# Sorting 65,536 edges by source on packed words: 15 of 16 merges of a bitonic sort carry one word per edge instead of two

## The chip, the cores and the metric

The kernel runs on one core of one Trainium2 chip. The metric is the device time of one execution in microseconds (us), the median of several executions. Engines are named as in the profile: PE (TensorE), DVE (VectorE), ACT (ScalarE), POOL (GpSimd), SP (SyncE, which here only issues DMAs).

## The reference

Four graph layers are applied one after another to node features `x` (100,000 nodes, 64 features) over 50,000 edges (`src`, `dst`, with `dst` sorted), each as `x = x + layer(relu(layernorm(x)))`. The second of them needs a softmax over the edges that share a *source*:

```python
src, dst = (edge_index[0], edge_index[1])
e = jax.nn.leaky_relu(h[src] @ a_src + h[dst] @ a_dst, ALPHA)
seg_max = jax.ops.segment_max(e, src, num_segments=num_nodes)
exp_e = jnp.exp(e - seg_max[src])
denom = jax.ops.segment_sum(exp_e, src, num_segments=num_nodes)
attention = exp_e / denom[src]
h_prime = jax.ops.segment_sum(attention[:, None] * h[src], dst, num_segments=num_nodes)
```

The edges arrive sorted by `dst`, so the kernel sorts them by `src` itself.

## The kernel before, in words

The program is a chain of blocks. A block opens a set of tiles and semaphores, gives each engine its own list of instructions, and ends with a barrier of all engines; nothing of the next block starts before it. The first block, `prologue_block` (tiles named `su_...`), prepares indices and weights. The second is `gat_block` "a" (tiles `a_...`), which gathers node rows by edge; its first instructions are the DMAs of SP at L712 and L717 and POOL's gathers at L755.

Inside the prologue, four strands run side by side:

- **DVE** first prepares masks (L268 to L306, L564 to L568) and then sorts. The sort is a bitonic network over `SORTED` = 65,536 slots, in tiles of 128 partitions by `SF` = 512 columns. `key` holds the source, `pay` the number of the edge, both as fp32, each in two copies used in turn. Merge k (k = 1 to 16) has k exchanges, 136 in all. Ahead of each merge a header of four instructions over 128x512 (L342 to L345) flips the keys' signs where the merge runs downwards, so that every exchange is the same: smaller value to the front. Each exchange is seven instructions over 128x256 (L325 to L331): a comparison and a difference of payloads, a minimum and a maximum of the keys, the product of comparison and difference, and two that move the payloads by it.
- **PE and ACT** serve the merges above 9 (`inner`), whose wide exchanges cross partitions. `turn_tiles` (L336) signals PE, which transposes `key` into the bank `bk` and `pay` into `bp` (L539), ACT copies both back (L526, L527), and DVE goes on. Each of the merges 10 to 16 has two such turns, 14 in all.
- **POOL** issues 392 indirect DMAs (L403), each of which scatters 128 single words into the table `XL`. They wait for masks of DVE (`dv`), and for the copy of the node table into `XL` (`xlc`). There are no data between them and the sort.
- **SP and ACT** issue loads and stores. SP stores the sorted keys and edge numbers (L464, L465) when DVE has signalled `sorted_` (L356), and then 18 small DMAs of weight parts (L471).

The block ends when all strands have ended: for DVE that is L383, behind the sort; for POOL the landing of its last scatter.

`ch(...)` is a helper: the instruction increments a semaphore, and DVE waits for that value before it goes on. In an exchange there are three such waits (behind L326, L329 and L331), in a header four.

Of the kernel before, what the change touches and what calls it, by code (L numbers as in the profile page):

```python
# [5 lines left out]
ALU = mybir.AluOpType  # L6
ACT = mybir.ActivationFunctionType
F32 = mybir.dt.float32
I32 = mybir.dt.int32
# [3 lines left out]
P = 128  # L13
N, D = 100000, 64
# [14 lines left out]
SORTED = 1 << (E - 1).bit_length()  # L29
SF = SORTED // P  # L30
SLAST = E - (P - 1) * EF
XW = D + 2
FAR = 1 << 23

# [158 lines left out]
def prologue_block(nc, a, T, C):  # L193

    with ExitStack() as ctx:
# [43 lines left out]
        tmp = [m.sb(f"tmp{i}", [P, SF // 2]) for i in range(3)]  # L239
        sign = m.sb("sign", [P, SF])  # L240
        bits = m.sb("bits", [P, SF], I32)
        place = m.sb("place", [P, SF], I32)
        srcs = m.sb("srcs", [P, SF], I32)
        eid = m.sb("eid", [P, SF], I32)
# [22 lines left out]
        def _(dve):  # L267
# [2 lines left out]
            nc.vector.memset(dstn[:, :], N)  # L270
            nc.vector.memset(C["at"][:, 0, EF - J:EF], 0)
            nc.vector.memset(C["at"][:, 1, EF - J:EF], N - 1)
            nc.vector.memset(sign[:, :], 1.0)
            nc.vector.memset(srcs[:, :], SKIP)
            nc.vector.memset(beyond[:, :], SKIP)
            nc.vector.memset(ewp[:, :], 0.0)
            nc.vector.memset(etp[:, :], 0)
# [32 lines left out]
            ch = Chain(dve, s_sort, 0)  # L310
            ch.at(0)
            dve.wait_ge(s_seed, 1)
            ch(v.tensor_copy(pay[0][:, :], place[:, :]))
            dve.wait_ge(s_ld, 16 * 2)
            dve.wait_ge(pads, 1)
            ch(v.tensor_copy(key[0][:, :], srcs[:, :]))
            cur, nt_, half = 0, 0, SORTED // P // 2

            def exchange(cur, d):
                a_ = lambda t: t[:, :].rearrange("p (g two d) -> p g two d", two=2, d=d)  # L320
                h_ = lambda t: t[:, :].rearrange("p (g d) -> p g d", d=d)
                ka, kb = a_(key[cur])[:, :, 0, :], a_(key[cur])[:, :, 1, :]
                pa, pb = a_(pay[cur])[:, :, 0, :], a_(pay[cur])[:, :, 1, :]
                nk, np_ = a_(key[1 - cur]), a_(pay[1 - cur])
                v.tensor_tensor(h_(tmp[0]), ka, kb, ALU.is_gt)  # L325
                ch(v.tensor_tensor(h_(tmp[1]), pb, pa, ALU.subtract))  # L326
                v.tensor_tensor(nk[:, :, 0, :], ka, kb, ALU.min)
                v.tensor_tensor(nk[:, :, 1, :], ka, kb, ALU.max)
                ch(v.tensor_tensor(tmp[2][:, :], tmp[0][:, :], tmp[1][:, :], ALU.mult))  # L329
                v.tensor_tensor(np_[:, :, 0, :], pa, h_(tmp[2]), ALU.add)  # L330
                ch(v.tensor_tensor(np_[:, :, 1, :], pb, h_(tmp[2]), ALU.subtract))  # L331
                return 1 - cur

            def turn_tiles(cur, n):

# [3 lines left out]

            for k in merges:  # L340

                ch(v.tensor_scalar(bits[:, :], place[:, :], k, 1, ALU.logical_shift_right, ALU.bitwise_and))  # L342
                ch(v.tensor_tensor(key[cur][:, :], key[cur][:, :], sign[:, :], ALU.mult))
                ch(v.tensor_scalar(sign[:, :], bits[:, :], -2.0, 1.0, ALU.mult, ALU.add))
                ch(v.tensor_tensor(key[cur][:, :], key[cur][:, :], sign[:, :], ALU.mult))  # L345
                if k > inner:
                    nt_ = turn_tiles(cur, nt_)
                    for j in range(k - 1, inner - 1, -1):
                        cur = exchange(cur, 1 << (j - inner))
                    nt_ = turn_tiles(cur, nt_)  # L350
                for j in range(min(k, inner) - 1, -1, -1):
                    cur = exchange(cur, 1 << j)

            if cur:
                ch(v.tensor_copy(key[0][:, :], key[1][:, :]))
# [120 lines left out]
        @block.scalar  # L476
        def _(act):
            act.wait_ge(pads, 1)
            act.dma_start(srcs[0:full, :], a["src"][0:full * SF].rearrange("(p f) -> p f", f=SF)).then_inc(s_ld, 16)
            act.dma_start(srcs[full:full + 1, 0:E - full * SF], a["src"][full * SF:E].unsqueeze(0)).then_inc(s_ld, 16)  # L480
            for c in range(1, 10, 2):
                act.dma_start(wide_rows(T["XL"], c), wide_rows(a["nodes"], c)).then_inc(xlc, 16)
            loads_ = 0

            def load(dst, src):
                act.dma_start(dst, src).then_inc(wl, 16)
                return 1
# [24 lines left out]
            for q in range(2):  # L512
                loads_ += load(C["a1"][:, q:q + 1], a["L1_gnn_a"][0, q * D:(q + 1) * D].unsqueeze(1))
            for q in range(4):
                loads_ += load(C["wflat"][:, q % 2, q // 2, :],
                          a["L2_gnn_weight"].rearrange("b i o -> (b i o)").rearrange("(q p i) -> q p i", p=P, i=D)[q])
            comp = a["w_comp_t"]
            for r in range(4):
                for q in range(4):
                    loads_ += load(C["cstk"][32 * r + 8 * q:32 * r + 8 * q + 8, 16 * q:16 * q + 16], comp)  # L520
            for name, of, H, W in (("att1b", "L0_gnn_att1", 8, 16), ("att2b", "L0_gnn_att2", 2, 64), ("att3b", "L3_gnn_att", 4, 16)):
                for h in range(H):
                    loads_ += load(C[name][h * W:(h + 1) * W, h:h + 1], a[of][h].unsqueeze(1))
            for n, cur in enumerate(current_at_turns()):
                act.wait_ge(s_tp, n + 1)
                nc.scalar.activation(key[cur][:, :], bk[:, :], ACT.Copy)  # L526
                nc.scalar.activation(pay[cur][:, :], bp[:, :], ACT.Copy).then_inc(s_tr, 1)  # L527
            act.wait_ge(wl, 16 * loads_)
            act.sem_inc(s_wr, 1)

        @block.tensor
        def _(pe):
            pe.wait_ge(s_id, 1)
            for n, cur in enumerate(current_at_turns()):
                pe.wait_ge(s_tq, n + 1)
                for tile_, bank in ((key[cur], bk), (pay[cur], bp)):
                    for b in range(SF // P):

                        last = nc.tensor.transpose(bank[:, b * P:(b + 1) * P], tile_[:, b * P:(b + 1) * P], C["ident"][:, :])  # L539
                last.then_inc(s_tp, 1)  # L540

            pe.wait_ge(s_ab, 1)
            for q in range(2):
                nc.tensor.matmul(pw[:, q * D:(q + 1) * D], ab[:, q, :], C["w1"][:, :], start=True, stop=True)
            nc.tensor.transpose(pt[:, :], C["w1"][:, :], C["ident"][0:D, 0:D])
            for q in range(2):
                last = nc.tensor.transpose(pf[:, q, :], C["wflat"][:, q, :, :].rearrange("p c i -> p (c i)"), C["ident"][:, :])
            last.then_inc(s_pe, 1)
# [1654 lines left out]
```

## Time and profile before

| | |
|---|---|
| median of 3 executions | 9188.93 us (9160.83 to 9189.82) |
| the profiled execution | 9215.03 us, of which the span is 9213.2 us |
| busy share of the span | DVE 70%, POOL 49%, PE 48%, ACT 31% |
| prologue block | 0 to 918.7 us of the span |
| DVE at 104.7 us | first instruction of the sort (L313) |
| DVE at 901.1 us | last instruction of the sort (L356) |

How to read it: the shares are means over 13 blocks with a barrier between each two. The change touches the first block alone, so what counts is which strand of that block ends last.

### The profile page before, as it was taken

The numbers are of one execution on the slowest core, as the hardware profiler recorded it, in microseconds if no ns is written. First come the engines' busy times: TensorE is split into PE (matmuls) and PEld (weight loads), VectorE is DVE, ScalarE is ACT, GpSimd is POOL, SyncE is SP. The second block draws the span as 40 slices with busy tenths as digits, with TensorE's granted clock in tenths as the row PEclk, the third lists the DMA queues.
The fourth block names the chain that finished last, engine by engine and source line by source line (L and its number), as shares of the span: only waits on it lengthen the run. The fifth ranks groups of instructions, "written<-read, shape, count | busy, mean of one in ns | idle before, by whom it ended". The sixth has DMA issues, their size and how long they took to land. (4 is left out here: it accounts for less than half of the span.)

```text
span 9213.2 us, 91644 instructions
## 1 busy us (share of the span) xinstructions
PE 4455.8 (48%) x13072; PEld 2477.6 (27%) x13072; DVE 6495.0 (70%) x20579; ACT 2837.8 (31%) x6952; POOL 4503.7 (49%) x4361
## 2 busy tenths in 40 slices
PE   0000556565566565776000988867756676720000
PEld 0000222222233333665000546623323333310000
DVE  4227789888576776877566998767868787878422
ACT  0000344443122222555343000134434444457200
POOL 3760666664666664554554000055445565623566
PEclk9999766666677766555555997578865555555555
DMA  5000333334333331111453002566634444433222
GB/s 150 1 1 4 73 78 84 79 79 69 74 73 73 72 74 41 36 36 46 88 100 81 1 4 83 146 109 128 127 79 88 88 92 84 94 99 123 74 79 74
DMA packets 910191, 686.98 MB, mean 75 GB/s; under 512 B 599695, under 2 KB 748972, under 8 KB 909450
## 3 DMA queue, kind: packets, MB, share of 16 engines
q1 hardware_dynamic: 515806, 377.81, 15.5%
q0 software_dynamic: 137984, 138.92, 12.0%
q10 hardware_dynamic: 256232, 168.62, 5.9%
q14 instruction: 138, 1.13, 0.0%
q8 instruction: 31, 0.51, 0.0%
HBM read 491.06 MB, written 227.24 MB: 78 GB/s over the span
## 5 line engine op out<-in xcount | busy, mean ns | idle before, releaser
L755 POOL DMA_INDIRECT a_xg<-t_XL,c_at x784 | 808.5, 1031 | 741.9 <-issue 292.6
L755 POOL DMA_INDIRECT g_xg<-t_D,c_at x784 | 784.2, 1000 | 630.8 <-DMA t_HN<-g_hn 305.9
L755 POOL DMA_INDIRECT b_xg<-t_H,c_at x784 | 815.5, 1040 | 494.1 <-issue 242.8
L1740 POOL DMA_INDIRECT f_dg<-t_D,c_at x392 | 371.3, 947 | 1286.7 <-POOLq L175 974.3
L1088 POOL DMA_INDIRECT t_RANK<-m_place,m_at x392 | 386.2, 985 | 393.9 <-DMA m_place<-t_POS 285.8
L1273 POOL DMA_INDIRECT l_d<-t_D,l_ix x392 | 387.8, 989 | 318.4 <-DVE l_xs L1289 136.8
L403 POOL DMA_INDIRECT t_XL<-su_pos,su_scatx x392 | 405.1, 1033 | 245.2 <-DMA t_XL<-in_nodes 126.1
L2108 POOL DMA_INDIRECT out<-o_y,o_ix x392 | 385.9, 984 | 260.7 <-issue 209.5
L539 PE MATMUL su_bk<-c_ident,su_key 128*128 128x128 f32 x56 | 15.6, 434 | 847.9 <-DVE su_tmp L336 847.9
L1010 PE MATMUL g_bank<-g_zt,c_att3r 64*128 64x512 f32 x196 | 200.1, 1123 | 414.1 <-DVE g_zt L800 238.1
L1322 ACT ACTIVATE l_hn<-l_xs,l_sm 128x64 f32<-128x64 f32 x784 | 265.0, 426 | 429.1 <-DVE l_sm L631 348.0
L1010 PE MATMUL a_bank<-a_zt,c_att1r 128*128 128x512 f32 x196 | 200.3, 1126 | 405.7 <-issue 217.0
L1010 PE MATMUL b_bank<-b_zt,c_att2r 128*128 128x512 f32 x196 | 192.4, 1084 | 369.6 <-DVE b_zt L796 202.5
L2084 DVE TENSOR_TENSOR o_t<-o_ag,c_k 128x256 f32<-128x256 f32 x98 | 41.9, 427 | 435.2 <-DMA o_x<-t_X 385.0
L1862 ACT ACTIVATE f_hn<-f_xs,f_bykind 128x64 f32<-128x64 f32 x784 | 265.0, 426 | 270.0 <-issue 169.2
L1363 PE MATMUL pr_prow<-c_ident,pr_col 128*1 128x128 f32 x2 | 0.6, 394 | 713.1 <-DVE pr_col L1381 713.1
L891 ACT ACTIVATE a_hn<-a_xg,a_sm 128x64 f32<-128x64 f32 x784 | 270.3, 427 | 242.9 <-DVE a_sm L631 128.7
L795 DVE TENSOR_TENSOR b_zt<-b_xl,b_bank 128x512 f32<-128x512 f32 x98 | 67.3, 687 | 373.5 <-ACT b_xl L919 124.3
L1987 POOL TENSOR_TENSOR n_x<-n_x,c_c 128x1280 f32<-128x1280 f32 (+1 forms) x40 | 157.1, 3932 | 320.7 <-DVE n_y L2017 251.0
L2030 ACT ACTIVATE n_h<-n_x,n_sm 128x64 f32<-128x64 f32 (+1 forms) x800 | 269.4, 426 | 131.1 <-DVE n_sm L631 131.1
L891 ACT ACTIVATE g_hn<-g_xg,g_sm 128x64 f32<-128x64 f32 x784 | 270.0, 427 | 122.3 <-DVE g_sm L631 86.8
L1442 PE MATMUL pb_sums<-pb_rhs,pb_lhs 128*128 128x392 f32 x784 | 260.1, 495 | 10.9 <-DVE pb_rhs L1433 10.9
(422 smaller groups left out, 15074.4 us busy)
## 6 DMA issues: line engine op xcount, KB each, us to landing
a_start<-t_START SPq DMA_DIRECT2D x98, 256.0 KB
t_XSD<-a_xg SPq DMA_DIRECT2D x98, 256.0 KB
t_H<-a_oE ACTq DMA_DIRECT2D x98, 256.0 KB
b_start<-t_START SPq DMA_DIRECT2D x98, 256.0 KB
l_xb<-t_XSD SPq DMA_DIRECT2D x49, 512.0 KB
f_rl<-t_REL SPq DMA_DIRECT2D x49, 512.0 KB
g_xb<-t_XSD SPq DMA_DIRECT2D x98, 256.0 KB
g_start<-t_START SPq DMA_DIRECT2D x98, 256.0 KB
```

The costliest lines, as they stand in the source:

```text
L403: nc.gpsimd.indirect_dma_start(lp, bass.IndirectOffsetOnAxis(ap=scatx[:, f:f + 1], axis=0), pos[:, f:f + 1].bitcast(F32), None, bounds_che ...
L755: nc.gpsimd.indirect_dma_start(xg[k][:, j, i, :], None, table, bass.IndirectOffsetOnAxis(ap=C["at"][:, i, n * J + j:n * J + j + 1], axis=0 ...
L891: last = f(hn[k][:, g // 2, g % 2, :], xg[k][:, g // 2, g % 2, 0:D], ACT.Relu, bias=sm[:, 5, g:g + 1], scale=sm[:, 4, g:g + 1])
L1010: mm(bS[:, :], att[:, :], zt[k][:, :], start=True, stop=True).then_inc(S["s"], 1)
L1088: nc.gpsimd.indirect_dma_start(rank, bass.IndirectOffsetOnAxis(ap=at[k][:, j:j + 1], axis=0), place[k][:, j:j + 1], None).then_inc(s_rank[ ...
L1273: nc.gpsimd.indirect_dma_start(d1[k][:, 0, j, :], None, T["D1"], bass.IndirectOffsetOnAxis(ap=ix[k][:, j:j + 1], axis=0)).then_inc(s_g[k], 16)
L1322: last = nc.scalar.activation(hn[k][:, g % 2, g // 2, :], xs[k][:, g // 2, g % 2, :], ACT.Relu, bias=sm[:, 5, g:g + 1], scale=sm[:, 4, g:g ...
L1442: nc.tensor.matmul(sums[:, :], lhs[c % SL][:, :], rhs[c % SL][:, :], start=(c == 0), stop=(c == EF - 1)).then_inc(s_mm, 1)
L1740: nc.gpsimd.indirect_dma_start(dg[k][:, u, j, :], None, T["D2"], bass.IndirectOffsetOnAxis(ap=C["at"][:, 0, (2 * n + u) * J + j:(2 * n + u ...
L1862: last = f(hn[k][:, g // J, g % J, c, :], xs[k][:, g // J, g % J, :], ACT.Relu, bias=by_kind[:, c, 1, g:g + 1], scale=by_kind[:, c, 0, g:g ...
L2030: last = f(h[k][0:np_, g, :], x3[k][0:np_, g, :], ACT.Relu, bias=sm[0:np_, 5, g:g + 1], scale=sm[0:np_, 4, g:g + 1])
L2108: nc.gpsimd.indirect_dma_start(out, bass.IndirectOffsetOnAxis(ap=ix[k][:, j:j + 1], axis=0), y[k][:, j, :], None, bounds_check=N - 1, oob_ ...
```

## The change

A source is below 2^17 and an edge number below 2^16, too much together for the 24 exact bits of an fp32 number. The packed word is therefore a bit pattern: the source less 50,000 (`HALF`), as a sign and a magnitude that is shifted up by 15 bits, with the lower 15 bits of the edge's number below it. Read as fp32, such patterns sort like the pair. The edge number's 16th bit is not in the word; it follows from which half of the slots the word is in, as long as the two halves have not been merged, that is up to the last merge. `unpack` restores key and payload ahead of merge 16. The flip of signs needs one multiplication per header instead of two, because the sign pattern is that of two merges together (`gray`).

```diff
+            ch(v.tensor_scalar(gray[:, :], place[:, :], 1, None, ALU.logical_shift_right))
+            ch(v.tensor_tensor(gray[:, :], gray[:, :], place[:, :], ALU.bitwise_xor))
...
+            ch(v.tensor_scalar(pay[0][:, :], srcs[:, :], -float(HALF), None, ALU.add))
+            v.tensor_scalar(sign[:, :], pay[0][:, :], 0.0, None, ALU.is_lt)
...
+            ch(v.tensor_tensor(key[0][:, :], bits[:, :].bitcast(F32), sign[:, :], ALU.mult))
...
+            def exchange_packed(cur, d):
+                (ka, kb), (lo, hi) = halves(key[cur], d), halves(key[1 - cur], d)
+                v.tensor_tensor(lo, ka, kb, ALU.min)
+                ch(v.tensor_tensor(hi, ka, kb, ALU.max))
+                return 1 - cur
...
+            def unpack(cur):
+
+                packed = key[cur][:, :].bitcast(I32)
+                v.tensor_scalar(srcs[:, :], place[:, :], 1 << LOWBITS, None, ALU.bitwise_and)
+                v.tensor_scalar(bits[:, :], packed, (1 << LOWBITS) - 1, None, ALU.bitwise_and)
+                v.tensor_scalar(eid[:, :], packed, LOWBITS, (1 << 16) - 1, ALU.logical_shift_right, ALU.bitwise_and)
+                ch(v.tensor_scalar(sign[:, :], key[cur][:, :], 0.0, None, ALU.is_lt))
+                v.tensor_copy(key[1 - cur][:, :], eid[:, :])
+                ch(v.tensor_scalar(sign[:, :], sign[:, :], -2.0, 1.0, ALU.mult, ALU.add))
+                v.tensor_tensor(pay[cur][:, :], bits[:, :], srcs[:, :], ALU.add)
+                ch(v.tensor_tensor(key[cur][:, :], key[1 - cur][:, :], sign[:, :], ALU.mult))
...
             for k in merges:
 
-                ch(v.tensor_scalar(bits[:, :], place[:, :], k, 1, ALU.logical_shift_right, ALU.bitwise_and))
-                ch(v.tensor_tensor(key[cur][:, :], key[cur][:, :], sign[:, :], ALU.mult))
+                ch(v.tensor_scalar(bits[:, :], gray[:, :] if k > 1 else place[:, :], max(k - 1, 1), 1,
+                                   ALU.logical_shift_right, ALU.bitwise_and))
                 ch(v.tensor_scalar(sign[:, :], bits[:, :], -2.0, 1.0, ALU.mult, ALU.add))
                 ch(v.tensor_tensor(key[cur][:, :], key[cur][:, :], sign[:, :], ALU.mult))
+                swap = exchange if k == merges[-1] else exchange_packed
+                if k == merges[-1]:
+                    unpack(cur)
...
-                nc.scalar.activation(key[cur][:, :], bk[:, :], ACT.Copy)
-                nc.scalar.activation(pay[cur][:, :], bp[:, :], ACT.Copy).then_inc(s_tr, 1)
+                last = nc.scalar.activation(key[cur][:, :], bk[:, :], ACT.Copy)
+                if n // 2 + 1 == len(turns):
+                    last = nc.scalar.activation(pay[cur][:, :], bp[:, :], ACT.Copy)
+                last.then_inc(s_tr, 1)
...
-                for tile_, bank in ((key[cur], bk), (pay[cur], bp)):
+                for tile_, bank in ((key[cur], bk), (pay[cur], bp))[:2 if n // 2 + 1 == len(turns) else 1]:
```

On DVE, at the start of the sort, one merge (header, then its exchange) and the header of the next stood so before, each row one instruction with its line, output and inputs, and the shape written:

```order
46 L342 TENSOR_SCALAR su_bits<-su_place 128x512
47 L343 TENSOR_TENSOR su_key<-su_key,su_sign 128x512
48 L344 TENSOR_SCALAR su_sign<-su_bits 128x512
49 L345 TENSOR_TENSOR su_key<-su_key,su_sign 128x512
50 L325 TENSOR_TENSOR su_tmp<-su_key 128x256
51 L326 TENSOR_TENSOR su_tmp<-su_pay 128x256
52 L327 TENSOR_TENSOR su_key<-su_key 128x256
53 L328 TENSOR_TENSOR su_key<-su_key 128x256
54 L329 TENSOR_TENSOR su_tmp<-su_tmp 128x256
55 L330 TENSOR_TENSOR su_pay<-su_pay,su_tmp 128x256
56 L331 TENSOR_TENSOR su_pay<-su_pay,su_tmp 128x256
57 L342 TENSOR_SCALAR su_bits<-su_place 128x512
```

and stand so now, with the last three rows of the packing ahead of them:

```order
51 L328 TENSOR_SCALAR su_sign<-su_sign 128x512
52 L329 TENSOR_TENSOR su_bits<-su_bits,su_srcs 128x512
53 L330 TENSOR_TENSOR su_key<-su_bits,su_sign 128x512
54 L376 TENSOR_SCALAR su_bits<-su_place 128x512
55 L378 TENSOR_SCALAR su_sign<-su_bits 128x512
56 L379 TENSOR_TENSOR su_key<-su_key,su_sign 128x512
57 L339 TENSOR_TENSOR su_key<-su_key 128x256
58 L340 TENSOR_TENSOR su_key<-su_key 128x256
59 L376 TENSOR_SCALAR su_bits<-su_gray 128x512
```

A merge of one exchange has gone from eleven instructions to five; the whole DVE program from 6371 rows to 5771.

On PE, the transposes of the prologue; before, the pair of the first two rows repeats 14 times:

```order
1 L539 MATMUL su_bk<-c_ident,su_key 128x128 x4
2 L539 MATMUL su_bp<-c_ident,su_pay 128x128 x4
3 L539 MATMUL su_bk<-c_ident,su_key 128x128 x4
4 L539 MATMUL su_bp<-c_ident,su_pay 128x128 x4
```

and now, up to the first matmul behind the sort:

```order
1 L578 MATMUL su_bk<-c_ident,su_key 128x128 x52
2 L578 MATMUL su_bp<-c_ident,su_pay 128x128 x4
3 L578 MATMUL su_bk<-c_ident,su_key 128x128 x4
4 L578 MATMUL su_bp<-c_ident,su_pay 128x128 x4
5 L583 MATMUL su_pw<-c_w,su_ab 128x64 x2
```

Twelve of the fourteen turns transpose `key` alone; the two of merge 16 transpose both, as before.

## Rows read from the trace of the kernel before

**Rows 1.** The page: the span, and busy shares in 40 slices of 230 us.

```profile
span 9213.2 us, 91644 instructions
...
DVE  4227789888576776877566998767868787878422
...
POOL 3760666664666664554554000055445565623566
```

**Rows 2.** Timeline of POOL: its last two scatters, and its first instruction of the next block.

```profile
658.29 1.09 POOL L403 DMA_INDIRECT t_XL<-su_pos,su_scatx  x1 [0.30 <-issue]
659.69 1.09 POOL L403 DMA_INDIRECT t_XL<-su_pos,su_scatx  x1 [0.30 <-issue]
919.43 0.97 POOL L755 DMA_INDIRECT a_xg<-t_XL,c_at  x1 [258.65 <-POOLq L175]
```

**Rows 3.** Timeline, the end of the block and the next one's first DMA.

```profile
901.08 0.43 DVE L356 CAST su_eid<-su_pay 128x512 int32<-128x512 f32 x1
...
905.13 5.70 SPq L471 DMA_DIRECT2D c_we1p<-su_wpart  x9
...
910.88 5.64 SPq L471 DMA_DIRECT2D c_we2p<-su_wpart  x9
...
918.72 0.32 SPq L712 DMA_DIRECT2D a_ext<-t_EWP  x1
```

**Rows 4.** By stretch of the prologue: stretch, length, each engine's busy us (instructions), PEclk, DMA share, GB/s.

```profile
core 0: us, PE busy (x) PEld busy (x) DVE busy (x) ACT busy (x) POOL busy (x), PEclk, DMA share, GB/s
136.60:181.60 45.00, 0.00 (x0) 0.00 (x0) 43.19 (x109) 0.00 (x0) 34.98 (x33) 1.00 0.60 133
181.60:661.00 479.40, 9.82 (x40) 7.85 (x40) 131.89 (x345) 5.43 (x10) 370.11 (x359) 1.00 0.02 1
661.00:685.40 24.40, 1.97 (x8) 1.57 (x8) 6.52 (x19) 1.09 (x2) 0.00 (x0) 1.00 0.00 0
685.40:901.10 215.70, 15.76 (x64) 12.56 (x64) 182.68 (x489) 8.68 (x16) 0.00 (x0) 1.00 0.00 0
901.10:918.70 17.60, 1.83 (x7) 1.27 (x7) 4.46 (x21) 0.00 (x0) 0.00 (x0) 1.00 0.09 30
```

**Rows 5.** Timeline of DVE, an exchange at about 200 us: start, duration, idle before it.

```profile
201.49 0.42 DVE L325 TENSOR_TENSOR su_tmp<-su_key 128x256 f32<-128x256 f32 x1 [2.04 <-remote]
...
204.29 0.43 DVE L327 TENSOR_TENSOR su_key<-su_key 128x256 f32<-128x256 f32 x1 [2.04 <-remote]
...
208.50 0.42 DVE L330 TENSOR_TENSOR su_pay<-su_pay,su_tmp 128x256 f32<-128x256 f32 x1 [3.11 <-remote]
...
211.29 0.42 DVE L325 TENSOR_TENSOR su_tmp<-su_key 128x256 f32<-128x256 f32 x1 [2.03 <-remote]
```

**Rows 6.** Timeline of DVE, an exchange at about 695 us.

```profile
694.21 0.43 DVE L325 TENSOR_TENSOR su_tmp<-su_key 128x256 f32<-128x256 f32 x1
694.55 0.42 DVE L326 TENSOR_TENSOR su_tmp<-su_pay 128x256 f32<-128x256 f32 x1
695.00 0.42 DVE L327 TENSOR_TENSOR su_key<-su_key 128x256 f32<-128x256 f32 x1
...
696.93 0.42 DVE L325 TENSOR_TENSOR su_tmp<-su_key 128x256 f32<-128x256 f32 x1
```

**Rows 7.** All of POOL's scatters: duration ns min/median/max, first and last start us.

```profile
L403 POOL DMA_INDIRECT t_XL<-su_pos,su_scatx x392: 966/972/1795, 136.6 to 659.7; - x196
```

**Rows 8.** Timeline, a header and a turn at about 710 us.

```profile
707.80 0.43 DVE L342 TENSOR_SCALAR su_bits<-su_place 128x512 int32<-128x512 int32 x1
708.26 0.69 DVE L343 TENSOR_TENSOR su_key<-su_key,su_sign 128x512 f32<-128x512 f32 x1
708.99 0.43 DVE L344 TENSOR_SCALAR su_sign<-su_bits 128x512 f32<-128x512 int32 x1
...
710.20 0.06 DVE L336 MEMSET su_tmp<- 128x1 f32 x1
...
711.22 1.06 PE L539 MATMUL su_bp<-c_ident,su_pay 128*128 128x128 f32 x4
712.32 0.60 ACT L526 ACTIVATE su_key<-su_bk 128x512 f32<-128x512 f32 x1 [31.64 <-PE su_bp L539]
712.82 0.59 ACT L527 ACTIVATE su_pay<-su_bp 128x512 f32<-128x512 f32 x1
713.44 0.42 DVE L325 TENSOR_TENSOR su_tmp<-su_key 128x256 f32<-128x256 f32 x1 [3.18 <-ACT su_pay L527]
```

**Rows 9.** Timeline of DVE: the longest idle time behind a turn in the sort.

```profile
446.93 0.42 DVE L325 TENSOR_TENSOR su_tmp<-su_key 128x256 f32<-128x256 f32 x1 [10.83 <-issue]
```

More of the change, by code:

```diff
@@ L31 @@
 SLAST = E - (P - 1) * EF
+HALF = N // 2
+LOWBITS = SORTED.bit_length() - 2
+LEAST = 1 << (23 - LOWBITS)
+NONE = HALF + 60000 - LEAST
 XW = D + 2
@@ L241, in prologue_block @@
         bits = m.sb("bits", [P, SF], I32)
+        gray = m.sb("gray", [P, SF], I32)
         place = m.sb("place", [P, SF], I32)
@@ L272, in _ @@
             nc.vector.memset(C["at"][:, 1, EF - J:EF], N - 1)
-            nc.vector.memset(sign[:, :], 1.0)
-            nc.vector.memset(srcs[:, :], SKIP)
+            nc.vector.memset(srcs[:, :], NONE)
             nc.vector.memset(beyond[:, :], SKIP)
@@ L312, in _ @@
             dve.wait_ge(s_seed, 1)
-            ch(v.tensor_copy(pay[0][:, :], place[:, :]))
+            ch(v.tensor_scalar(gray[:, :], place[:, :], 1, None, ALU.logical_shift_right))
+            ch(v.tensor_tensor(gray[:, :], gray[:, :], place[:, :], ALU.bitwise_xor))
             dve.wait_ge(s_ld, 16 * 2)
             dve.wait_ge(pads, 1)
-            ch(v.tensor_copy(key[0][:, :], srcs[:, :]))
-            cur, nt_, half = 0, 0, SORTED // P // 2
+            ch(v.tensor_scalar(pay[0][:, :], srcs[:, :], -float(HALF), None, ALU.add))
@@ new lines, in _ @@
+            v.tensor_scalar(sign[:, :], pay[0][:, :], 0.0, None, ALU.is_lt)
+            ch(v.tensor_scalar(pay[1][:, :], pay[0][:, :], -1.0, float(LEAST - 1), ALU.mult, ALU.add))
+            ch(v.scalar_tensor_tensor(bits[:, :], pay[0][:, :], float(LEAST), pay[1][:, :], ALU.add, ALU.max))
+            v.tensor_scalar(srcs[:, :], place[:, :], (1 << LOWBITS) - 1, None, ALU.bitwise_and)
+            ch(v.tensor_scalar(bits[:, :], bits[:, :], LOWBITS, None, ALU.logical_shift_left))
+            v.tensor_scalar(sign[:, :], sign[:, :], -2.0, 1.0, ALU.mult, ALU.add)
@@ new lines, in _, with halves @@
+            ch(v.tensor_tensor(bits[:, :], bits[:, :], srcs[:, :], ALU.bitwise_or))
+            ch(v.tensor_tensor(key[0][:, :], bits[:, :].bitcast(F32), sign[:, :], ALU.mult))
+            cur, nt_ = 0, 0
+            def halves(t, d):
+                by = t[:, :].rearrange("p (g two d) -> p g two d", two=2, d=d)
+                return by[:, :, 0, :], by[:, :, 1, :]
+            def exchange_packed(cur, d):
[3 more added lines that the diff above has]
+                return 1 - cur
@@ L319, in exchange @@
             def exchange(cur, d):
-                a_ = lambda t: t[:, :].rearrange("p (g two d) -> p g two d", two=2, d=d)
                 h_ = lambda t: t[:, :].rearrange("p (g d) -> p g d", d=d)
-                ka, kb = a_(key[cur])[:, :, 0, :], a_(key[cur])[:, :, 1, :]
-                pa, pb = a_(pay[cur])[:, :, 0, :], a_(pay[cur])[:, :, 1, :]
-                nk, np_ = a_(key[1 - cur]), a_(pay[1 - cur])
+                (ka, kb), (pa, pb) = halves(key[cur], d), halves(pay[cur], d)
+                nk, np_ = halves(key[1 - cur], d), halves(pay[1 - cur], d)
@@ L325, in exchange @@
                 v.tensor_tensor(h_(tmp[0]), ka, kb, ALU.is_gt)
                 ch(v.tensor_tensor(h_(tmp[1]), pb, pa, ALU.subtract))
-                v.tensor_tensor(nk[:, :, 0, :], ka, kb, ALU.min)
-                v.tensor_tensor(nk[:, :, 1, :], ka, kb, ALU.max)
+                v.tensor_tensor(nk[0], ka, kb, ALU.min)
+                v.tensor_tensor(nk[1], ka, kb, ALU.max)
                 ch(v.tensor_tensor(tmp[2][:, :], tmp[0][:, :], tmp[1][:, :], ALU.mult))
-                v.tensor_tensor(np_[:, :, 0, :], pa, h_(tmp[2]), ALU.add)
@@ L331, in exchange @@
-                ch(v.tensor_tensor(np_[:, :, 1, :], pb, h_(tmp[2]), ALU.subtract))
+                v.tensor_tensor(np_[0], pa, h_(tmp[2]), ALU.add)
+                ch(v.tensor_tensor(np_[1], pb, h_(tmp[2]), ALU.subtract))
                 return 1 - cur
+            def unpack(cur):
[8 more added lines that the diff above has]
+                ch(v.tensor_tensor(key[cur][:, :], key[1 - cur][:, :], sign[:, :], ALU.mult))
@@ L348, in _ @@
                     for j in range(k - 1, inner - 1, -1):
-                        cur = exchange(cur, 1 << (j - inner))
+                        cur = swap(cur, 1 << (j - inner))
                     nt_ = turn_tiles(cur, nt_)
                 for j in range(min(k, inner) - 1, -1, -1):
-                    cur = exchange(cur, 1 << j)
+                    cur = swap(cur, 1 << j)
             if cur:
```

## The prediction

> **What bounds the kernel now.** I read the page's slices first: in the first four, DVE shows 4, 2, 2 and 7 tenths and POOL 3, 7, 6 and 0 [rows 1], so in the prologue POOL's strand ends before DVE's, and DVE has its lowest shares just while POOL works. The timeline at the block's end says by how much. POOL's last scatter is issued at 659.69 and ends at 660.8, and POOL's next instruction starts at 919.43, behind an idle time of 258.65 us at the barrier [rows 2]. The sort ends with L356 at 901.08, SP's small DMAs run from 905.13 to 916.5, and the next block starts at 918.72 [rows 3]. So from 661 to 918.7 the program waits for the sort and its tail of 17.6 us alone. What the change is worth is the distance from 918.7 down to whatever ends last once the sort is short.
>
> The stretches of the prologue show how slow the sort is, and that it has two paces [rows 4]. From 685.4 to 901.1 DVE issues 489 instructions in 215.7 us, one per 0.44 us (turns included), and is busy throughout. From 181.6 to 661 it issues only 345 in 479.4 us, one per 1.39 us, and is 28% busy. In an exchange of the slow stretch [rows 5] DVE idles 2.04, 3.11 and 2.03 us at its three waits: the starts lie 2.80, 4.21 and 2.79 us apart, with two, three and two instructions in between. That is 1.40 us **per instruction**, not per wait: 7 x 1.40 = 9.80 us an exchange, against 696.93 - 694.21 = 2.72 us in the fast stretch [rows 6]. The slow pace begins at about 181.6 us and outlasts POOL's issue to 685.4, where 136.6 + 392 x 1.40 = 685.4 also ends: as if each scatter, from the first at 136.6 [rows 7], held a slot of 1.40 us, in which DVE is let through one instruction. POOL's own last scatters lie 1.40 us apart too [rows 2]. What the slot is, the trace doesn't say; I use its measured price.
>
> **The change, part by part.**
> - *Packed exchanges*: 120 of 136. In the fast pace the second instruction starts 0.34 us behind the first, and the next group 0.45 us behind that [rows 6]: 0.79 us instead of 2.72. In the slow pace two instructions are 2.8 us instead of 9.8.
> - *Headers*: three instructions instead of four. L342 and L344 cost 0.46 us each to the next start, L343 0.73 [rows 8]: 1.65 us fast instead of 2.4, 4.2 slow instead of 5.6.
> - *Turns*: 710.20 to 713.44 is 3.24 us [rows 8]. Without the payload's transposes (0.9, of the 1.06 from 711.22 on) and its copy back (0.5), some 1.8 us, in 12 of 14.
> - *Packing* adds 11 instructions over 128x512 for 2, four of two tensors at 0.73 and seven of one at 0.34 to 0.46 [rows 8]: about 5.8 us. *Unpacking* adds 8: about 4.5 us fast, 11 slow.
> - No DMA, no wait between engines and no order on POOL or SP is changed. Merge 16 keeps all its 112 exchange instructions.
>
> **The new sort in time.** It starts at 104.7 as before; packing until 110.5. Merges 1 to 9: 9 x 1.65 + 45 x 0.79 = 50.4, to 160.9. Merge 10: 1.65 + 2 x 1.8 + 7.9 = 13.1, to 174.0. By 181.6 merge 11 is past its header, both turns and three exchanges. From there, by instructions: 16 for its other eight exchanges; 4 x (3 + 2) + 54 x 2 = 128 for merges 12 to 15; 3 + 8 + 2 + 112 = 125 for merge 16; one for L356. That is 270 x 1.39 = 375 us, to 557. The pace of 1.39 was measured with five turns inside, so turns are paid. The 20 instructions of DVE behind the sort cost 28 us more at that pace, and SP's 12 us behind them: the sort's strand ends at about **600** instead of 918.7.
>
> That is before POOL's strand, which the change doesn't touch: the bound moves to the scatters. They are issued until 660.8, and the slots end at 685.4. I take the later one, because POOL's part in the barrier comes behind its scatters, in the same queue that held DVE's signals back. With about 1.3 us for the barrier, as the sum for before has it (916.5 and the landing of a small DMA to 918.7), the next block starts at 686.7. Saved: 918.7 - 686.7 = 232 us. The rest of the program is the same instructions behind a barrier, so nothing else moves. Against its own time the profiled execution becomes 9215 - 232 = 8983; it stood 26 us above the median, and 9188.9 - 232 = **8957**.
>
> Bounds: the sort would have to reach 668 before its tail of 17.6 matters, that is (668 - 181.6) / 270 = 1.80 us an instruction instead of 1.39. If the ten turns left were paid on top, at the 3.24 us of the fast pace, the strand would end at 632, still hidden; at the longest idle time behind a turn, 10.83 us [rows 9], at 708, and the gain would be 210 us. That time stood behind the second of two turns close together, with eight transposes each; the new turns have four, so I take none of it. If waits and not instructions set the pace (9.8 / 3 = 3.27 us a wait), an exchange is 3.27 instead of 2.8, 29 us more over 62 exchanges: hidden as well. So the end of the sort doesn't enter the sum; POOL's end does, between 660.8 and 685.4.
>
> **The lock between DVE and POOL.** Beside a DVE in full work (136.6 to 181.6) POOL issues 33 scatters in 45 us, one per 1.36 us; beside a stalled DVE, 359 in 479.4, one per 1.34 [rows 4]. The packed exchanges have the same density of work as the old ones in the first stretch, and less of it in all. The Trainium skill, page SBUF — State Buffer, section "Who interferes with whom", warns of the reverse of hidden work: an operation of VectorE that uses both ports locks GpSimd out, so that it cannot write descriptors, and a DMA of some 620 ns then takes some 3100. By that figure 392 scatters would take 1215 us and the block would end near 1352, an estimate that would make the kernel slower; the rows above give 1.36 us a scatter at full density, and the sum goes by them.
>
> **Rivals.**
> 1. *POOL is free at its last issue* (0.19). The barrier opens when the last scatter lands, about 663 to 665: 918.7 - 665 = 254 us saved, and up to 6 more if POOL goes back from 1.40 to 1.27 us a scatter (the median 0.97 [rows 7] and 0.30) once DVE is idle (some 50 scatters by 0.12). That gives 8935 to 8929. For it: the waits are for the DMAs' landings. Against: 661 to 685.4 still has 19 instructions of DVE at 1.28 us each [rows 4], so something of POOL's was outstanding; and such a rest would slow the first gathers of the next block.
> 2. *The sort stays last* (0.05): the slow pace is above 1.80 us for the new mix, for instance because integer operations over 128x512 take two slots. At 2.2 us, 181.6 + 594 + 17.6 + 15 is a block of 808, or 9078.
> 3. *No gain* (0.05): the slow pace exists only while a trace is recorded. The timed sort would then end at 181.6 + 364 x 0.44 + 215.7 = 557 and be hidden already: 9189 again. Against it: the timed median would then lie 232 us under the profiled execution, and it lies 26 under. The Trainium skill, page NOTIFIC — the notification-queue block, section 7.1, says that a full internal queue of trace records holds an engine back; that would be this rival's mechanism, and no row here names it.
> 4. *Slower* (0.05): the scatters slow down and decide. The block lasts as long as now if a scatter takes (918.7 - 136.6) / 392 = 1.995 us; the longest of the 392 took 1.795 [rows 7], with 0.30 between two 2.095, and at that price all of them end at 958: 9228. It takes DVE work that blocks POOL in nearly every issue; only the 2-input and int32 instructions of packing are new, and they are over before 136.6.
>
> **How the numbers follow.** The forecast, 8957, has 0.66; its own range is 8940 to 8975, for the spread of the three executions. Rival 1 reaches down to 8929, with that spread 8915. The range 8915 to 8990 holds both (0.85) with little of rival 2. All of them are faster by over 0.3%, about what a measurement of this kernel can tell from no change: 0.66 + 0.19 + 0.05 = 0.90; no change 0.05, slower 0.05.
>
> **What would show it.** In the new trace: the fast pace until about 181; packed pairs 2.8 us apart until the sort's end; L356's successor near 557; SP's small DMAs over by about 600; POOL's last scatter still near 660; the first row of the next block at 665 to 687, with DVE waiting there and not POOL; and all later blocks as long as before. I am wrong if POOL's scatters move, if the pace per instruction isn't 1.4 us, or if the next block gives back time in its first 100 us.

## The result and the profile after

The changed kernel takes 8961.46 us, median of 4 runs (8932.29 to 8976.25); the kernel before, run beside it, 9177.9 us (4 runs, 9160.83 to 9189.82). The ratio is 0.9752 [0.9734, 0.977] (in brackets, here and below, the 95% interval). The forecast was 8957. The profiled execution took 8960.75 us with a span of 8958.6, 254.6 less than before.

First the page of the changed kernel: span and slices, which answer to [rows 1].

```profile
span 8958.6 us, 90936 instructions
...
DVE  4216888995777767885668998577768878878322
...
POOL 3776666655766745554550000354356555523566
```

DVE now shows 4, 2 and 1 tenths, and the next block is there in the fourth slice; the fast part of the sort, which filled the fourth slice of before with 7 tenths, is gone. POOL works in the first three as before. Next the stretches of its prologue, with the columns of [rows 4].

```profile
core 0: us, PE busy (x) PEld busy (x) DVE busy (x) ACT busy (x) POOL busy (x), PEclk, DMA share, GB/s
134.20:181.60 47.40, 3.32 (x12) 2.15 (x12) 37.02 (x94) 1.79 (x3) 36.71 (x36) 1.00 0.58 126
181.60:562.00 380.40, 13.97 (x52) 9.57 (x52) 102.10 (x272) 7.54 (x13) 292.69 (x289) 1.00 0.02 1
562.00:598.40 36.40, 1.84 (x7) 1.27 (x7) 4.67 (x21) 0.00 (x0) 28.78 (x26) 1.00 0.06 15
598.40:657.90 59.50, 0.00 (x0) 0.00 (x0) 0.00 (x0) 0.00 (x0) 46.40 (x44) 1.00 0.02 0
657.90:676.10 18.20, 0.00 (x0) 0.00 (x0) 1.46 (x3) 0.00 (x0) 0.99 (x2) 1.00 0.02 5
```

From 181.6 on, DVE issues 272 instructions in 380.4 us, 1.40 us each, where before it was 345 at 1.39. The sort ends at 562.2 and its tail at 598.4. Then only POOL works, for 59.5 us, until its last scatter ends at 657.9. The timeline shows two packed exchanges of DVE in the slow stretch, then the end of the block (start, duration, instruction, idle time before it); these answer to [rows 5], [rows 2] and [rows 3].

```profile
192.20 0.42 DVE L340 TENSOR_TENSOR su_key<-su_key 128x256 f32<-128x256 f32 x1
194.65 0.43 DVE L339 TENSOR_TENSOR su_key<-su_key 128x256 f32<-128x256 f32 x1 [2.04 <-remote]
195.00 0.42 DVE L340 TENSOR_TENSOR su_key<-su_key 128x256 f32<-128x256 f32 x1
197.45 0.43 DVE L339 TENSOR_TENSOR su_key<-su_key 128x256 f32<-128x256 f32 x1 [2.04 <-remote]
...
562.17 0.43 DVE L393 CAST su_eid<-su_pay 128x512 int32<-128x512 f32 x1 [2.04 <-issue]
...
573.41 11.70 SPq L508 DMA_DIRECT2D c_we1p<-su_wpart  x9
...
585.90 12.46 SPq L508 DMA_DIRECT2D c_we2p<-su_wpart  x9
...
655.42 1.09 POOL L440 DMA_INDIRECT t_XL<-su_pos,su_scatx  x1 [0.30 <-issue]
656.82 1.09 POOL L440 DMA_INDIRECT t_XL<-su_pos,su_scatx  x1 [0.30 <-issue]
674.49 0.49 DVE L804 MEMSET a_r<- 128x513 f32 x1 [86.97 <-PEq L199]
675.02 0.97 POOL L794 DMA_INDIRECT a_xg<-t_XL,c_at  x1 [17.10 <-issue]
...
676.11 3.50 SPq L751 DMA_DIRECT2D a_ext<-t_EWP  x1
```

The exchange takes 2.80 us (192.20, 195.00). Where POOL waited 258.65 us for the block's end, it now waits 17.10 and DVE waits 86.97. The bound of the prologue has passed from the sort to the scatters. The scatters themselves hardly moved; the group of all of them answers to [rows 7].

```profile
L440 POOL DMA_INDIRECT t_XL<-su_pos,su_scatx x392: 966/972/1792, 134.2 to 656.8; - x196
```

So the prologue saved 918.7 - 676.1 = 242.6 us. The rest of the program did not stay as it was. In the windows of the later stages before and after, the first fence is of before, the second of after; the rows are the blocks behind the prologue, then the relation block alone (tiles named f_), then what follows it.

```profile
918.70:5991.40 5072.70, 2943.72 (x9227) 1759.78 (x9227) 3922.31 (x12019) 1554.57 (x3827) 2405.62 (x2361) 0.64 0.31 68
5991.40:6761.70 770.30, 557.60 (x1568) 227.55 (x1568) 564.14 (x1822) 323.68 (x883) 371.38 (x393) 0.83 0.62 118
6761.70:9213.20 2451.50, 925.14 (x2158) 467.02 (x2158) 1593.89 (x5642) 943.10 (x2213) 1319.62 (x1208) 0.50 0.36 88
```

```profile
676.10:5714.30 5038.20, 2950.75 (x9227) 1763.61 (x9227) 3920.61 (x12016) 1554.81 (x3827) 2411.53 (x2359) 0.64 0.32 68
5714.30:6504.40 790.10, 565.62 (x1568) 227.45 (x1568) 565.59 (x1822) 323.67 (x883) 370.27 (x392) 0.82 0.60 116
6504.40:8958.60 2454.20, 925.48 (x2158) 467.32 (x2158) 1593.67 (x5642) 942.47 (x2213) 1321.28 (x1208) 0.50 0.35 88
```

The span's difference is -242.6 in the prologue, -34.5 in the first stretch, +19.8 in the relation block and +2.7 in the rest: -254.6. The -34.5 is no gain of the change that I can defend: a second profile of the kernel before (before_again, below) has a span 43 us shorter with the same instructions. What the change does cost in that stretch, some 10 us at its start, is hidden in it (see why the prediction was right). The +19.8 is in part an effect of the change, as the last set of runs shows: the block loads more code.

### The profile page after: what moved, and what is told of

The parts are those of the page before. It is cut to its first block and busy times, and to the rows that moved or that the text cites. A ratio compares the mean times of both kernels' runs of the same rounds, so it can differ in the third digit from the quotient of the medians.

```text
span 8958.6 us, 90936 instructions
## 1 busy us (share of the span) xinstructions
PE 4461.0 (50%) x13024; PEld 2471.4 (28%) x13024; DVE 6269.5 (70%) x19979; ACT 2831.6 (32%) x6940; POOL 4510.6 (50%) x4361
## 5 line engine op out<-in xcount | busy, mean ns | idle before, releaser
L1481 PE MATMUL ps_sums<-ps_rhs,ps_lhs 128*128 128x392 f32 x784 | 261.3, 497 | 8.4 <-DVE ps_rhs L1472 8.4
```

The lines of the kernel that those rows point to most:

```text
L1481: nc.tensor.matmul(sums[:, :], lhs[c % SL][:, :], rhs[c % SL][:, :], start=(c == 0), stop=(c == EF - 1)).then_inc(s_mm, 1)
```

## The experiments

There were three sets of runs, each on one chip: the kernel before took 9087.84 us beside the first set, 8208.17 beside the second and 9196.24 beside the third. "The second chip" below is the chip of the second set. The kernels of the first set and half_partitions ran once each and are read by their prologue only, since a total moves by tens of us: third_instruction took 8824.95 us and two_waits 8862.13, though the prologue of the first is 16 us longer.

**Whose price is the slow pace?** Both kernels with no scatter at all; their output lacks what the scatters write, and their totals (9278.43 and 9110.09 us) are not compared, since the later blocks then gather other rows.

```diff
-            for b in range(EF // 8):
+            for b in range(0):
...
-            for k in range(4):
-                pool.wait_ge(s_sc[k], 16 * 8 * chunks_of(k, 4, EF // 8))
```

old_no_scatter (the kernel before without its scatters):

> The kernel before, with the 392 scatters of POOL in the prologue left out (the table then holds the default edge number everywhere, so later gathers go to one row and only the prologue is read). If POOL's scatters make DVE's slow pace: no slow stretch at all, an exchange is 2.72 us throughout, the sort ends at 105 + 136 x 2.72 + 16 x 2.4 + 14 x 3.24 = 559 and the next block starts near 577. If the slow pace comes of something else (the silence of the other DMAs after 181 us, or instruction supply): still about 1.39 us an instruction after 181, and the sort ends near 900 or later.

new_no_scatter (the changed kernel without them):

> The changed kernel, with the 392 scatters left out (only the prologue is read). Theory: POOL's strand is what bounds the changed prologue, and it also slows the sort. Then the sort ends at 174 + 5 x (1.65 + 3.6) + 65 x 0.79 + 56 = 308 instead of 562, and the next block starts near 326. If the packed sort itself still bound the block, the next block would start near 674 less nothing.

The windows of old_no_scatter and of new_no_scatter from 181.6 to the sort's end:

```profile
181.60:558.00 376.40, 27.54 (x112) 21.97 (x112) 318.53 (x846) 15.21 (x28) 0.00 (x0) 1.00 0.00 0
```

```profile
181.60:307.00 125.40, 12.86 (x48) 8.87 (x48) 99.72 (x267) 6.95 (x12) 0.00 (x0) 1.00 0.00 0
```

That is 0.44 and 0.47 us per instruction. The sorts end at 558.5 and 307.2, the next blocks start at 576.1 and 324.9, each within 2 us of what was expected. The slow pace belongs to the scatters and to nothing in the sort: removing them took 343 us off the old sort (901.1 to 558.5) and 255 off the new (562.2 to 307.2). The two ends with scatters are from the chip of the first result; on the chip of this set two_waits, below, has the new sort end at 562.9.

**Per instruction or per wait?** third_instruction puts a third, tiny instruction without a wait into each packed exchange; two_waits keeps two instructions and puts a wait between them.

```diff
                 v.tensor_tensor(lo, ka, kb, ALU.min)
+                v.memset(tmp[1][:, 0:1], 0.0)
```

> The changed kernel, with one more DVE instruction in each packed exchange: a memset of one column between minimum and maximum, and no further wait. If the slow pace is a price per instruction (1.40 us): packed exchanges lie 4.2 us apart in the slow stretch instead of 2.8, the sort ends 62 to 65 x 1.4 = about 90 us later, near 652, and with the tail of 36 us seen in the changed kernel the sort's strand is last again: next block near 688 instead of 674. If it is a price per wait or per element written: exchanges stay 2.8 us apart, the sort ends near 568, block unchanged at 674.

```diff
-                v.tensor_tensor(lo, ka, kb, ALU.min)
+                ch(v.tensor_tensor(lo, ka, kb, ALU.min))
```

> The changed kernel, with a wait of its own behind the minimum too: two instructions and two waits in each packed exchange. Price per instruction: still 2.8 us an exchange in the slow stretch, the sort ends near 568 (6 us from the fast stretch), block unchanged at 674. Price per wait (2.8 us for each wait as now): 5.6 us an exchange, the sort ends 180 us later, and the next block starts near 750.

The timeline of DVE in third_instruction, then in two_waits, at about 305 us:

```profile
307.26 0.43 DVE L339 TENSOR_TENSOR su_key<-su_key 128x256 f32<-128x256 f32 x1 [3.43 <-remote]
307.62 0.42 DVE L341 TENSOR_TENSOR su_key<-su_key 128x256 f32<-128x256 f32 x1
307.64 0.06 DVE L340 MEMSET su_tmp<- 128x1 f32 x1
311.46 0.43 DVE L339 TENSOR_TENSOR su_key<-su_key 128x256 f32<-128x256 f32 x1 [3.43 <-remote]
```

```profile
304.63 0.43 DVE L339 TENSOR_TENSOR su_key<-su_key 128x256 f32<-128x256 f32 x1 [0.97 <-DVE su_key L340]
306.03 0.43 DVE L340 TENSOR_TENSOR su_key<-su_key 128x256 f32<-128x256 f32 x1 [0.97 <-DVE su_key L339]
307.43 0.43 DVE L339 TENSOR_TENSOR su_key<-su_key 128x256 f32<-128x256 f32 x1 [0.97 <-DVE su_key L340]
```

A memset of 0.06 us makes the exchange 4.20 us long instead of 2.80; a second wait leaves it at 2.80. The price is 1.40 us for every instruction, whatever its size, and none for a wait. It is paid at the next wait: the three instructions of an exchange still start within 0.4 us, and the idle time behind them grows from 2.04 to 3.43 us. In third_instruction the sort ends at 665.0 (expected: about 652; I had counted too few of the added instructions into the slow stretch: its window holds 346 against 272, and 74 x 1.40 = 104), and its next block starts 14.6 us later than that of after. The window up to the sort's end, and from the timeline the next block's first DMA:

```profile
181.60:665.00 483.40, 15.08 (x56) 10.28 (x56) 106.59 (x346) 8.14 (x14) 364.94 (x356) 1.00 0.02 1
```

```profile
690.69 0.32 SPq L752 DMA_DIRECT2D a_ext<-t_EWP  x1
```

That is the bound from the other side: a sort that ends about 100 us later becomes the last strand again. In two_waits the sort ends at 562.9 and the next block starts at 674.4, as in after.

**How far may the sort grow?** The second set of runs repeats the changed kernel and moves the unpacking to merge 15 or 13, so that two or four merges work on two words. half_partitions lets each scatter write from 64 partitions (half of the scattered rows are missing), to ask whether the 1.40 us follow the scatter's size.

```diff
-                swap = exchange if k == merges[-1] else exchange_packed
-                if k == merges[-1]:
+                swap = exchange if k >= 15 else exchange_packed
+                if k == 15:
...
-                if n // 2 + 1 == len(turns):
+                if turns[n // 2] >= 15:
```

> The changed kernel once more, on the chip of the next runs: ratio to the kernel before 0.972 to 0.978; the next block's first DMA at 674 to 677 us.

> The changed kernel with unpacking ahead of merge 15 instead of 16, so that merge 15 is on two words too: 15 exchanges of seven instructions instead of two, 75 more instructions, all in the slow stretch. Price per instruction: the sort ends 75 x 1.40 = 105 us later, at 667; with the tail of 25.7 us that the run with a third instruction showed, the next block starts at 693, 17 to 19 us later than in the changed kernel (0.2%). If the sort did not matter at all any more: unchanged, 674. If the whole saving were in proportion to the instructions left out (244 us for 597): 31 us later.

> The changed kernel with unpacking ahead of merge 13: merges 13 to 16 on two words, 210 more instructions. Slots end at 134 + 392 x 1.40 = 683; up to there 86 of the 210 are paid at 1.40, the other 124 at 0.42: the sort ends at 683 + 52 = 735, the next block starts at 753, 79 us later than in the changed kernel (ratio to the kernel before some 0.984). In proportion to instructions it would be 86 us later: only the run with merge 15 tells these apart.

```diff
-                    nc.gpsimd.indirect_dma_start(lp, bass.IndirectOffsetOnAxis(ap=scatx[:, f:f + 1], axis=0),
-                                                 pos[:, f:f + 1].bitcast(F32), None, bounds_check=N * XW - 1,
+                    nc.gpsimd.indirect_dma_start(lp, bass.IndirectOffsetOnAxis(ap=scatx[0:64, f:f + 1], axis=0),
+                                                 pos[0:64, f:f + 1].bitcast(F32), None, bounds_check=N * XW - 1,
```

> The changed kernel with each scatter over 64 of the 128 partitions (half of the edge numbers are not written; only the prologue is read). If the slot of 1.40 us is the DMA's descriptors (128 of them): the slot halves to 0.70, the sort ends near 182 + 270 x 0.70 = 371 plus turns, some 390, and POOL goes at its issue time, at most 1.27 us each, so the next block starts near 635 to 650. If the slot is a price per scatter instruction: 1.40 as before, sort ends at 562, next block near 674.

All of these expectations took for granted that the slow pace is there, and on this chip it is not. after_again, the same kernel as after, in its timeline and its window from 181.6 to the sort's end:

```profile
250.12 1.16 POOL L440 DMA_INDIRECT t_XL<-su_pos,su_scatx  x1 [0.30 <-issue]
250.47 0.42 DVE L339 TENSOR_TENSOR su_key<-su_key 128x256 f32<-128x256 f32 x1
250.81 0.42 DVE L340 TENSOR_TENSOR su_key<-su_key 128x256 f32<-128x256 f32 x1
251.26 0.43 DVE L339 TENSOR_TENSOR su_key<-su_key 128x256 f32<-128x256 f32 x1
```

```profile
181.60:308.00 126.40, 12.86 (x48) 8.86 (x48) 100.71 (x267) 6.95 (x12) 97.46 (x96) 1.00 0.02 1
```

An exchange takes 0.79 us beside the scatters, and 267 instructions take 126.4 us, as in new_no_scatter. The results: after_again 8241.84 us, ratio **1.0043 [1.0026, 1.0059]**; unpack_15 8194.95, 0.9983 [0.9974, 0.9993]; unpack_13 8203.14, 0.999 [0.9981, 1.0]. Their sorts end at 308.4, 340.7 and 398.3, all far ahead of the last scatter at 640.7, 645.0 and 648.1, and the next blocks start at 652.5, 656.8 and 659.9. There the prologue has, as it seems, nothing for the change to win (no trace of the kernel before was taken on that chip), and the whole kernel is 0.4% slower. half_partitions says nothing of the slow pace for the same reason: its scatters, issued 1.21 us apart instead of 1.27, end 23 us earlier (617.2).

**Where do the 0.4% come from?** Stage by stage, after_again and unpack_15 differ in the relation block: 733 us against 679. There the page's part on DMA queues, over that block's window, shows this row for after_again first and unpack_15 second (queue, packets, MB, share of the engines):

```profile
q14 instruction: 55, 0.45, 0.2%
```

```profile
q14 instruction: 15, 0.12, 0.1%
```

The queue's name says that these are loads of code: in after_again five packets in each round of the block's loop, in unpack_15 hardly any behind its start. The waits of DVE in that window, in after_again and then in unpack_15 (what waited for what: us in total, times, longest), show idle time that goes with them:

```profile
DVE f_d2b L1841 <- issue: 34.3, 8, 5.1
...
DVE f_o L1845 <- issue: 21.3, 9, 3.5
```

```profile
DVE f_d2b L1841 <- issue: 3.9, 9, 0.5
...
DVE f_o L1845 <- issue: 1.1, 1, 1.1
```

That is 55.6 us against 5.0, where DVE waits for nothing that the profile shows; the block is 54 us longer. unpack_13 sides with unpack_15: 15 packets and 679 us. On the chip of the first result it is the same: 15 packets before, 55 after, and DVE's wait at L1841 is 32.8 us after. The third set of runs tests whether the place of DVE's code decides. pad_dve adds 80 one-column memsets at the start of DVE's program and changes nothing else; pad_pe_act lengthens the programs of PE and ACT ahead of that loop (the payload is turned in merge 15 too) and leaves DVE's as it is.

```diff
+            for i in range(80):
+                nc.vector.memset(tmp[1][:, i:i + 1], 0.0)
```

> The changed kernel with 80 memsets of one column on DVE ahead of its wait for the loads, where it idles until 95 us; they shift all later DVE code by 80 instructions and do nothing else. If DVE's loop in the relation block is fetched anew in each round because of where it lies: fetches there go from 55 back to 15, DVE's idle time for issue there from 56 to about 5 us, and the kernel becomes 50 to 55 us faster than the changed one on a chip without the slow pace (ratio to before about 0.998), some 20 us faster on one with it. If it is PE's or ACT's loop: 55 fetches, as the changed kernel.

```diff
-                if n // 2 + 1 == len(turns):
+                if turns[n // 2] >= 15:
```

> The changed kernel with payload transposed and copied back in the turns of merge 15 too, as the run that unpacks at 15 has it, with DVE's code unchanged: 8 more transposes on PE, 2 more copies on ACT. If DVE's loop is what is fetched anew: 55 fetches in the relation block and the time of the changed kernel. If it is PE's or ACT's: 15 fetches and 50 us less.

Two unchanged kernels ran beside them:

> The kernel before, for its trace on the chip of the next runs. Two cases, by whether this chip shows the slow pace of 1.40 us an instruction beside POOL's scatters. With it: as in the first trace, next block near 918. Without it: an exchange is 2.72 us throughout, the sort ends near 559, the scatters are issued until about 645 and bound the block, and the next block starts near 655. The relation block has 15 instruction fetches in either case.

> The changed kernel. With the slow pace: next block near 675, ratio 0.975. Without it: next block near 653, no gain there, and the relation block with its 55 instruction fetches costs 50 to 55 us: ratio 1.004 to 1.007.

| run | ratio to before | next block starts | code packets in relation block | relation block, us |
|---|---|---|---|---|
| before_again (one run, 9171.72 us) | | 917.5 | 15 | 777.5 |
| after_third | 0.9735 [0.9706, 0.9764] | 674.6 | 55 | 784.7 |
| pad_dve | 0.9736 [0.9709, 0.9762] | 675.8 | 15 | 779.9 |
| pad_pe_act | 0.9771 [0.9742, 0.98] | 677.2 | 55 | 795.1 |

Eighty idle instructions on DVE bring the 15 packets back, and shifting PE and ACT does not: it is DVE's loop that is loaded again, and its place decides. Its place, and not how short the program ahead is: against the changed kernel 75, 80, 210 and 600 more instructions on DVE (unpack_15, pad_dve, unpack_13, the kernel before) give 15 packets, none (after) and 120 (third_instruction) give 55.

In time the 15 packets brought nothing here: 8954.46 us for pad_dve beside 8947.50 for after_third, where some 20 us less were expected. Of the eight profiles with the slow pace and a complete prologue, the three with 15 packets have relation blocks of 770.3, 777.5 and 779.9 us, the five with 55 have 777.5, 784.7, 789.7, 790.1 and 795.1: some 11 us in the mean, less than the 34 us between the fastest and the slowest of the four runs of after_third. DVE's idle time at the two lines is gone in pad_dve too (4.9 us; 56.9 in after_third), but it then waits longer elsewhere: at L1823 31.3 us until a DMA of `t_H` ended, where after_third has 2.6 at the same instruction. That most of the 55 us are hidden behind such waits where the pace is slow is read from these rows and not tested.

## Why the prediction was right, point by point

- **The sort bounds the prologue before; the bound moves to the scatters.** Shown by after, where POOL works alone for the last 59.5 us, and from both sides: new_no_scatter opens at 324.9, third_instruction at 690.7.
- **The slow pace is the scatters', 1.40 us per instruction and not per wait.** Shown by the four kernels of the first set. The sort's end came at 562.2 instead of 557: 272 instructions instead of 270 at 1.40 instead of 1.39. The end of its strand, forecast at about 600, came at 598.4. None of this entered the sum, as the forecast said; it only had to stay under 657.9.
- **The end of POOL's strand** was a term that was mis-sized. The sum had the next block at 686.7, where slots of 1.40 us would have ended; rival 1 had it at 663 to 665, at the last landing. It came at 676.1, 10.6 us before the one and 11 behind the other. The slots, counted from the first scatter of this trace, would have ended at 134.2 + 548.8 = 683.0, so POOL doesn't wait for all of them; nor is the way from the last scatter to the next block as short as 1.3 us of barrier. On the second chip, without any slow pace, POOL's first gather is issued 11.5 us behind the end of its last scatter; here 17.1. What fills these was not taken apart; the next point has what is left of the slots.
- **Nothing else moves** was the step that failed, in two places. The first is the next block. The prediction called itself wrong if that block gave back time in its first 100 us, and it does. The timeline of DVE there, in the kernel before and then in the changed one:

```profile
933.43 0.17 DVE L628 TENSOR_TENSOR a_sm<-a_sm 128x8 f32<-128x8 f32 x1
933.63 0.17 DVE L629 SCALAR_TENSOR_TENSOR a_sm<-a_sm 128x8 f32<-128x8 f32 x1
...
940.71 1.11 DVE L607 BATCH_NORM_STATS2 a_bn<-a_xg 128x6 f32<-128x64 f32 x8 [3.31 <-DMA a_xg<-t_XL,c_at]
```

```profile
696.57 0.17 DVE L667 TENSOR_TENSOR a_sm<-a_sm 128x8 f32<-128x8 f32 x1 [1.22 <-DVE a_sm L665]
697.97 0.17 DVE L668 SCALAR_TENSOR_TENSOR a_sm<-a_sm 128x8 f32<-128x8 f32 x1 [1.23 <-DVE a_sm L667]
...
708.47 0.17 DVE L670 SCALAR_TENSOR_TENSOR a_sm<-a_sm 128x8 f32<-128x8 f32 x1 [1.23 <-issue]
```

  The same two instructions lie 0.20 us apart before and 1.40 after, and the second batch of statistics starts 22.0 us behind the block's first DMA before (940.71) and 32.4 after (708.55, right behind the last row shown). It is the same in all traces: 22 us where the sort ended last (before, before_again, third_instruction), where the scatters were left out, and on the second chip; 32 to 34 us in the five traces with the slow pace where the scatters ended last. So the slow pace runs on through the barrier, and at that point about as much is paid back as the prologue had given more than forecast. Over the whole block it stands out little: 1359 to 1365 us in those five traces, 1347 to 1361 in the three where the sort ended last. The gathers are not slowed: they are issued 1.25 us apart in both kernels.

  The second is the code. Behind the barrier stand the same instructions, but DVE's program ahead of them is shorter by 600 instructions (20579 to 19979 of DVE), and the relation block's loop loads code again in every round. The block was 54 us longer on the second chip (after_again beside unpack_15), 5 in the third set (after_third beside pad_dve) and 20 in the first result, each from two traces.
- **The net figure** has luck in it. The medians fell by 216 us where 232 were forecast. The median of the kernel before came out 11 us lower with its fourth run, at 9177.9 instead of the 9188.9 that the forecast subtracts from, and what the prologue gave more is offset by what the blocks behind it lost. The mechanism of the prologue was foreseen; that 8961 lies within 5 us of 8957 was not earned.
- **Rival 3** (no gain, because the slow pace exists only in recorded executions) is refuted where the slow pace is: the timed medians fell by 216 us, and by 249 in the third set. But its arithmetic, a sort that is hidden already, describes the second chip. There the old sort would have ended near 558.5 (old_no_scatter) or little later, before the last scatter at 641. That is inferred; no trace of the kernel before was taken on that chip. Rival 2 is refuted by the 1.40 us, rival 4 by the longest of the scatters, 1.792 us.
- **The lock.** At DVE's densest, 36 scatters took 47.4 us, 1.32 us each; beside 0.79 us exchanges on the second chip 96 took 126.4 us, again 1.32 each. The Trainium skill, page SBUF — State Buffer, has the 3.1 us of the prediction's estimate for a DMA beside a `tensor_copy` (section "A bandwidth-pool intuition that's wrong (but worth ruling out)"), and says in the section "Who interferes with whom" that `tensor_tensor` has no 2-port mode. The exchanges are `tensor_tensor`, so the estimate of 1352 asked more than the page says, and that they do not block the scatters agrees with it. A faint effect is left: on the second chip the last scatter comes 4.3 and 7.4 us later when DVE has one or three more merges on two words.
- **A slip of the working.** Under rival 4 the integer and 2-input instructions that are new are said to be over before 136.6; those of `unpack` come ahead of merge 16, in the slow stretch. It changed nothing: the longest scatter took 1.792 us.

Open is why one chip has the slow pace and another has not, and what the slot of 1.40 us is. It is not the program: after and after_again are the same kernel, all four profiles of the second set lack the pace, and every other profile with scatters has it. Each set ran on one chip at one time, so what else differs between them was not told apart. On the second chip the other blocks whose gathers POOL issues are faster too (the first 1284 to 1287 us against 1347 to 1366 elsewhere), while the four blocks without them (267, 270, 349 and 444 us) are alike everywhere.

The best version depends on the chip. pad_dve matches the changed kernel where the pace is slow and was not run where it isn't; unpack_15 was 0.2% faster than the kernel before and 0.6% faster than the changed one on the second chip and was not run on the others.

## What to carry to other kernels

Before costing a stage by durations, divide its time by its instructions and look at what runs beside it: here an engine at 28% busy was bound by a price per instruction that another engine's indirect DMAs set, and fewer instructions, not cheaper ones, removed it. A gain that rests on such a price should be measured on more than one chip, since it was 2.5% and 2.7% here (first result and third set) and a loss of 0.4% on the second chip. When a program gets shorter, count the code loads of the loops behind the change before saying that nothing else moves, and look whether what bounded the stage before is over when the next one starts.

## What the runs showed of the hardware

- Beside POOL's indirect DMAs, an instruction of DVE costs 1.40 us on some chips, also a memset of 0.06 us, and the pace holds on into the next block when the scatters end last; the nine small DMAs of SP in that stretch took 11.70 and 12.46 us instead of 5.70 and 5.64 [rows 3]. On another chip neither the sort nor the whole kernel (8208 instead of 9178 us) shows it.
- The same loop loads 15 or 55 packets of code, depending on how many instructions DVE's program has ahead of it, and not in the order of that number; the block with 55 is up to 54 us longer, in 49 tiles of work.
- POOL's scatters too can lie 1.40 us apart, but not all through the slow stretch: from 181.6 to 562.0 they are 1.32 us apart in the mean, and on the second chip 1.27 once the sort is over. In after they run at 1.40 from 622 on, behind some 15 us at 1.27. That isn't DVE's doing, which had long been idle.
